# One core, six layers: sums turned by VectorE in two attention layers, projections two batches wide, loads reordered

## Time and profile before

| | |
|---|---|
| median of 3 runs | 1397.02 us (1395.74 to 1397.70) |
| profiled execution, its own time | 1397.33 us |
| its span in the trace | 1395.6 us |
| PE busy | 1329.5 us (95%) |
| DVE busy | 994.2 us (71%) |
| ACT busy | 898.1 us (64%) |
| POOL busy | 603.0 us (43%) |
| mean granted TensorE clock | 0.995 of full speed |

### The profile page before, as it was taken

One profiled execution on the slowest core, in us unless ns is written; L12 is line 12 of the kernel. 1 busy time (PEld: TensorE's weight loads), 2 busy tenths in 40 slices (PEclk: granted clock), 3 DMA queues, 4 the chain that ended last, 5 costly groups with the idle time before them and its releaser, 6 DMA issues.

```text
span 1395.6 us, 46148 instructions
## 1 busy us (share of the span) xinstructions
PE 1329.5 (95%) x20076; PEld 1138.8 (82%) x20076; DVE 994.2 (71%) x1842; ACT 898.1 (64%) x1519; POOL 603.0 (43%) x767
## 2 busy tenths in 40 slices
PE   5999999999999999999999999999999999899997
PEld 4777888777887878888788878888999999778885
DVE  4778777888788777767776788886664446767774
ACT  4777777777777756666566776776434435667764
POOL 4944544576644643443334342222686665111100
PEclk9999999999999999999999999999999999999999
DMA  7211100010100000000000110000000000001000
GB/s 283 76 31 35 31 13 10 24 31 25 38 9 9 10 25 3 3 2 2 3 2 25 33 31 16 9 9 24 9 9 1 2 1 15 10 32 39 17 25 32
DMA packets 16609, 35.11 MB, mean 25 GB/s; under 512 B 2071, under 2 KB 7447, under 8 KB 15895
## 3 DMA queue, kind: packets, MB, share of 16 engines
q1 hardware_dynamic: 16407, 32.16, 7.1%
HBM read 27.96 MB, written 4.19 MB: 23 GB/s over the span
## 4 chain that ended last, share of the span: by engine, by line
PE 67%; DVE 14%; ACT 8%; POOL 5%; issue 3%; DMA 2%; SPq 0%; DVEq 0%; POOLq 0%; ACTq 0%
DVE s_nm L1101 9%; PE ps L717 8%; PE ps L782 8%; PE ps L744 6%; PE ps L796 6%; PE ps L810 6%; PE ps L606 5%; PE ps L659 5%; PE ps L761 5%; PE ps L631 4%; ACT s_PU L952 4%; PE ps L618 4%; PE ps L595 2%; PE ps L722 2%; DVE s_KH L1058 2%
## 5 line engine op out<-in xcount | busy, mean ns | idle before, releaser
L1101 DVE TENSOR_REDUCE s_nm<-ps 128x8 fp32r<-128x960 f32 (+1 forms) x352 | 395.8, 1168 | 88.4 <-PE ps L659 51.0
L952 ACT ACTIVATE s_PU<-ps 120x1024 f32<-120x1024 f32 (+1 forms) x288 | 280.6, 1024 | 105.5 <-PE ps L722 105.3
L717 PE MATMUL ps<-s_Qs,s_KH 32*120 32x256 f32 (+2 forms) x4608 | 184.8, 288 | 6.4 <-ACT s_PU L952 2.6
L1225 POOL TENSOR_TENSOR s_xs<-s_xs,s_rowv 128x512 f32<-128x512 f32 x96 | 123.9, 1291 | 151.8 <-ACT s_nt L857 133.6
L717 PEld LDWEIGHTS ps<-s_Qs,s_KH 32*120 32x120 f32 (+1 forms) x4608 | 151.5, 181 | 28.4 <-issue 5.1
L1254 POOL TENSOR_SCALAR s_rs<-s_mv 128x2 f32<-128x2 f32 x96 | 23.2, 242 | 325.4 <-DVE s_mv L1138 319.8
L961 ACT ACTIVATE s_Os<-ps 128x512 f32<-128x512 f32 x160 | 95.0, 598 | 102.8 <-PE ps L744 64.2
L782 PE MATMUL ps<-s_W,s_oT 128*128 128x256 f32 x960 | 135.3, 291 | 5.2 <-DVE s_oT L1030 3.5
L606 PE MATMUL ps<-s_xT,s_W 128*128 128x256 f32 x960 | 135.9, 292 | 3.1 <-POOL s_xT L1231 2.8
L744 PE MATMUL ps<-s_PU,s_Vp 120*32 120x256 f32 x2048 | 129.5, 384 | 9.2 <-ACT s_PU L952 7.2
L782 PEld LDWEIGHTS ps<-s_W,s_oT 128*128 128x128 f32 x960 | 120.0, 190 | 16.8 <-DVE s_oT L1030 7.0
(11 more groups left out here) (96 smaller groups left out, 2554.4 us busy)
## 6 DMA issues: line engine op xcount, KB each, us to landing
s_cf<-ctx_t SPq DMA_DIRECT2D x32, 240.0 KB, 2.6
s_ws<-weights SPq DMA_DIRECT2D x28, 256.0 KB, 2.7
s_nt<-x_t SPq DMA_DIRECT2D x16, 256.0 KB, 2.6
s_xs<-x_nat SPq DMA_DIRECT2D x4, 1024.0 KB, 11.3
out<-s_xs SPq DMA_DIRECT2D x16, 256.0 KB, 2.0
s_rowv<-rows SPq DMA_DIRECT2D x6, 512.0 KB, 3.9
s_mi<-mask SPq DMA_DIRECT2D x8, 120.0 KB, 3.4
s_who<-who SPq DMA_DIRECT2D x1, 128.0 KB, 3.2
```

What stands on the lines that cost most here:

```text
L717: e.matmul(banks[j][0:n, wide * x:wide * x + wide], kz[row[j], lk, g, c, k0:k0 + n], q[row[j], lq, g, qs_], start=(x == 0 and y_ == 0), st ...
L952: t = e.activation(P_of(i, k)[0:n, :, :], pair("B", i, k)[0:n, :, :], ACT.Exp, scale=0.25)
L1101: e.tensor_reduce(o, v, AX.X, ALU.max, negate=True).then_inc(sem["max"])
L1225: e.tensor_tensor(xs[:, b, :, :], xs[:, b, :, :], row2(layer, 0), ALU.add).then_inc(sem["pool"])
```

## The change

In CROSS and L3 the sums no longer go through PE to be turned. DVE reads each half of PV out of PSUM and turns it in blocks of 32 x 32 (X), which puts 32 rows of each head on partitions; it takes the reciprocals of both halves at once (rec); POOL multiplies all 16 heads (nmul, one 128 x 512 operation); DVE turns back by 32 x 32 blocks out of SBUF (turn, two operations of 128 x 256); then OTh, OTl, O as before, but OTh and OTl read `s_On` in SBUF instead of PSUM. The rows of the two output matrices are permuted on the host (`mixed`). PVe, ON, ONe and OT are gone from these layers.

From CROSS on, T, Q and F1 work for two batches at once: Q is 12 matmuls of 512 columns for a pair, F1 four stages of 12 such matmuls, F2 four stages of 24 matmuls of 256 columns. `s_xT` and `s_Qs` are laid out for pairs.

The weights' low and high parts lie in ten places of one matrix each (three of four matrices before), and a matrix may be prepared when the one that had its place has been read. The high-part buffers change: K0 has 1 instead of 2, `s_oT` 1 instead of 2, `s_Os` 2 whole ones instead of 3 halves, Q 4 instead of 3. The planner waits with the four loads of `x` and with L1's weights; `WANT` has other numbers throughout and `STAY` is 1.453 instead of 0.236, so the order of all layers differs.

```diff
...
+TWOS = ("CROSS", "FFN", "L3")
+TURNED = ("CROSS", "L3")
...
-WSLOT = {n: k % 3 for k, n in enumerate(SETS)}
+
+MATRICES = [(n, m) for n in SETS for m in range(4)]
+PLACE = {x: k % 10 for k, x in enumerate(MATRICES)}
...
-            ON=(3.22, 2.87, 3, 2.88, 0, -1.81), ONe=(1.73, 1.71, -1.22, -2.11, 0, 0.18), OT=(4.46, -4.46, 2.98, 2.5, 0, 3.93),
...
+            exp=(0.82, 14.91, -1.61, 4.93, 0, -24.67), cap=-14.72, PV=(2.7, -1.45, 1.33, 5.16, 0, 6.91), X=(0, 0, 0, -15.84, 0, 2.3),
...
-STAY = 0.236
+STAY = 1.453
...
-        self.ring = {"Q": Slots(3), "KH": Slots(2), "K0": Slots(2), "PU": Slots(7), "Vp": Slots(2), "cT": Slots(2),
-                     "xT": Slots(2), "nt": Slots(2), "ws": Slots(2), "cf": Slots(1), "Os": Slots(3), "On": Slots(1), "oT": Slots(2), "nm": Slots(2), "mT": Slots(2),
+        self.ring = {"Q": Slots(4), "KH": Slots(2), "K0": Slots(1), "PU": Slots(7), "Vp": Slots(2), "cT": Slots(2),
+                     "xT": Slots(2), "nt": Slots(2), "ws": Slots(2), "cf": Slots(1), "Os": Slots(2), "Rc": Slots(2), "On": Slots(1), "oT": Slots(1), "nm": Slots(2), "mT": Slots(2),
...
         if layer == "FFN":
-            for u in range(2):
-                add("PE", "F1", u, after=[x_t] + [("Wl", "F1", m) for m in range(4)],
...
+            for u in range(4 if i == pair else 0):
+                add("PE", "F1", u, after=[x_t, ("Wl", "F1", u)],
+                    rings=[("S", ("F1", i, u), [("Fv", i, 2 * u + 1)]), ("PU", ("F", i, u), [("Hl", i, u)]),
                            ("KH", ("H", i, u), [("F2", i, u)])])
...
+            turned = layer in TURNED
             for hf in range(2):
...
+                    + ([("PV", i, 0)] if hf else []), long=1.36 if self_ else None,
+                    rings=[("MI", ("PV", i, hf), [("X" if turned else "PVe", i, hf)])]
+                    + ([] if hf else [("Os", i, [("turn", i, 0)] if turned else [("ON", i, 0), ("ON", i, 1)])]))
+                if turned:
+                    add("DVE", "X", hf, after=[("PV", i, hf)])
+                else:
+                    add("ACT", "PVe", hf, after=[("PV", i, hf)])
+                    add("PE", "ON", hf, after=[("PVe", i, hf)] + ([("ON", i, 0)] if hf else []),
+                        rings=[("MI", ("ON", i, hf), [("ONe", i, hf)])] + ([] if hf else [("On", i, [("OT", i, 0)])]))
...
+            if turned:
+                add("DVE", "rec", after=[("X", i, 0), ("X", i, 1)], rings=[("Rc", i, [("nmul", i, 0)])])
+                add("POOL", "nmul", after=[("rec", i, 0)])
+                add("DVE", "turn", after=[("nmul", i, 0)], rings=[("On", i, [("OTl", i, 0)]), ("oT", i, [("O", i, 0)])])
+            else:
...
             add("DVE", "OTl", after=[("OTh", i, 0)])
...
-        p.add("SP", "x", k, want=-1 + 1.2 * k)
+        p.add("SP", "x", k, want=-1 + 1.2 * k, after=[("A", 4 * k - 4, 0)] if k else [("K", 0, 0)])
...
-            p.add("SP", "ws", layer, m, want=at, rings=[("ws", (layer, m), [(rest_of(layer), layer, m)])])
+            p.add("SP", "ws", layer, m, want=at, after=[("A", 4 + m, 0)] if layer == "L1" else [], rings=[("ws", (layer, m), [(rest_of(layer), layer, m)])])
...
             def Q(i):
-                m, layer = bankM("Q", i), layer_of(i)
...
                 w.wait_ge(*w_ready(layer, 0))
                 for g in range(2):
                     for c, (cw, cx) in enumerate(PARTS):
                         for k in range(2):
-                            t = e.matmul(m[:, g * 256:g * 256 + 256], wv(layer, cw, 0)[:, k, 128 * g:128 * g + 128], xT_of(i)[:, cx, k, :],
+                            t = e.matmul(v[:, g, :], wv(layer, cw, 0)[:, k, 128 * g:128 * g + 128], xT_of(i)[:, cx, k, :],
                                          start=(c == 0 and k == 0), stop=(c == 2 and k == 1))
...
             def F1(i, u):
-                v, x = pair("F1", i, u), xT_of(i)
...
-                    o = v[:, mt % 4 // 2, 256 * (mt % 2):256 * (mt % 2) + 256]
+                w.wait_ge(*w_ready("F1", u))
+                for h in range(2):
                     for c, (cw, cx) in enumerate(PARTS):
                         for k in range(2):
-                            t = e.matmul(o, wv("F1", cw, mt // 2)[:, k, 128 * (mt % 2):128 * (mt % 2) + 128], x[:, cx, k, :],
+                            t = e.matmul(v[:, h, :], wv("F1", cw, u)[:, k, 128 * h:128 * h + 128], xT_of(i)[:, cx, k, :],
                                          start=(c == 0 and k == 0), stop=(c == 2 and k == 1))
                 t.then_inc(sem["F1"])
...
+                if layer_of(i) in TURNED:
+                    w.wait_ge(sem["turn"], nth("turn", i))
+                    src = On[slot("On", i)][:, :, :].rearrange("p a n -> p (a n)")
...
             def OTlo(i):
...
-                e.tensor_tensor(o[:, 1, :, :].rearrange("p a n -> p (a n)"), bankM("OT", i),
-                                o[:, 0, :, :].bitcast(f32).rearrange("p a n -> p (a n)"), ALU.subtract).then_inc(sem["OTl"])
+                src = On[slot("On", i)][:, :, :].rearrange("p a n -> p (a n)") if layer_of(i) in TURNED else bankM("OT", i)
+                e.tensor_tensor(o[:, 1, :, :].rearrange("p a n -> p (a n)"), src, o[:, 0, :, :].bitcast(f32).rearrange("p a n -> p (a n)"),
+                                ALU.subtract).then_inc(sem["OTl"])
...
+            def X(i, hf):
+
+
+                for x in sums_free(i):
+                    w.wait_ge(*x)
+                w.wait_ge(sem["PV"], nth("PV", i, hf))
+                e.transpose(Os_of(i, hf).rearrange("p g n -> p (g n)"), bankM("PV", i, hf)).then_inc(sem["X"])
+
+            def rec(i):
...
+                e.reciprocal(Rc[slot("Rc", i)][:, :].rearrange("p (h o) -> p h o", o=1), o[:, :, 16:17]).then_inc(sem["rec"])
...
+            def turn(i):
+
+                for x in On_free(i):
+                    w.wait_ge(*x)
+                w.wait_ge(sem["pool"], pool_ops["nmul", i, 0])
+                o = Os[slot("Os", i)]
+                for hf in range(2):
+                    t = e.transpose(On[slot("On", i)][:, hf, :], o[:, 2 * hf:2 * hf + 2, :, 0:16].rearrange("p g m c -> p m g c"))
+                t.then_inc(sem["turn"])
...
+            def nmul(i):
+
+                o = Os[slot("Os", i)][:, :, :, :].rearrange("p g m c -> p (g m) c")
+                w.wait_ge(sem["rec"], nth("rec", i))
...
+                rc = Rc[slot("Rc", i)][:, :].rearrange("p (h o) -> p h o", o=1)
+                e.tensor_tensor(o[:, :, 0:16], o[:, :, 0:16], rc.to_broadcast([128, 32, 16]), ALU.mult).then_inc(sem["pool"])
+
...
+    def mixed(w):
+
+        return w.reshape(2, 2, 4, 16, D).transpose(0, 2, 1, 3, 4).reshape(D, D)
...
```

More of the change, by code:

```diff
@@ L37 @@
+LONG = dict(mci=.5, xT=.6, cT=.6, mi=.6, ws=.6, row=.6, x=.6, out=.6, bo=1.3, N=.72, T=.88, Th=.95, Tl=1.13, Xl=2.6, Q=2.62, Qh=.98, Ql=1.24, K=1.35, K0=.87,
             Kh=1.17, Kl=1.25, V=1.43, Ve=.67, Ch=.5, Cl=1.25, mf=.3, A=.69, max=1.07, M=.22, mTe=.28, B=.95, exp=.91, cap=.67, PV=.87,
-            PVe=.48, ON=.44, ONe=.64, OT=.44, OTh=.48, OTl=.62, O=1.43, y=.6, st=1.05, rs=1.6, ln=.72, lng=2.6, F1=2.86, Fa=.72, Fv=.79,
+            X=.62, rec=.36, nmul=1.3, turn=.68, PVe=.48, ON=.44, ONe=.64, OT=.44, OTh=.48, OTl=.62, O=1.43, y=.6, st=1.05, rs=1.6, ln=.72, lng=2.6, F1=2.62, Fa=.49, Fv=.62,
@@ L276, in make_plan @@
-            last = ("F2", i, 1)
-        else:
-            add("PE", "Q", after=[x_t, (rest_of(layer), layer, 0)],
-                rings=[("MI", ("Q", i, 0), [("Ql", i, 0)]), ("Q", i, [("B", i, u) for u in range(units(i))])])
-            add("ACT", "Qh", after=[("Q", i, 0)] + ([("wa", layer, 0)] if FOLDED[layer] else []))
-            add("DVE", "Ql", after=[("Qh", i, 0)])
+                add("PE", "F2", u, after=[("Hl", i, u), ("Wl", "F2", u)] + ([("F2", i, u - 1)] if u else []),
+                    rings=[] if u else [("MI", ("F2", x, 0), [("y", x, 0)]) for x in two])
@@ new lines, in make_plan @@
+            last = ("F2", pair, 3)
+        else:
+            if i == pair:
+                add("PE", "Q", long=2.62 if len(two) == 2 else 1.43, after=[x_t, (rest_of(layer), layer, 0)],
+                    rings=[(bank, ("Q", i, 0), [("Ql", i, 0)])] + [("Q", x, [("B", x, u) for u in range(units(x))]) for x in two])
+                add("ACT", "Qh", long=LONG["Qh"] if len(two) == 2 else .74, after=[("Q", i, 0)] + ([("wa", layer, 0)] if FOLDED[layer] else []))
+                add("DVE", "Ql", long=LONG["Ql"] if len(two) == 2 else .8, after=[("Qh", i, 0)])
@@ L306, in make_plan @@
                     add("DVE", "max", 2 * u + q, after=[("A", i, u)])
+            for u in range(1, units(i)):
+                p.stages["A", i, u].after.append(("A", i, 0))
             add("PE", "M", after=[("max", i, k) for k in range(2 * units(i))],
@@ L322, in make_plan @@
[L322 to L327 removed]
+                add("PE", "PV", hf, after=[("cap" if self_ else "exp", i, k) for k in half_pairs(i, hf)] + [("Ve", first, 0)]
+                    + ([("PV", i, 0)] if hf else []), long=1.36 if self_ else None,
```

(14 more changed lines are left out.)

338 lines of the change are left out of this document (194 added, 144 removed).

## The result

The changed kernel takes 1372.97 us (median of 4 runs, 1371.68 to 1375.82) against 1397.36 of the kernel before in the same session: ratio 0.983, interval 0.9813 to 0.9848. That is 24.4 us less; 40 were forecast. The profiled execution took 1375.82, the slowest of the four; its span is 1374.1, 21.5 shorter than before.

The account below looks back on a forecast made before the run. PE, busy 95%, was taken to set the pace. CROSS −16.0, L3 −17.2, F1 −8.6, tiling +4.8 and start −3.0 sum to −40.0: 1397.3 becomes 1357 us, range 1335 to 1386.

Parts of the forecast that it names:

- Rival A: In CROSS, DVE operations within SBUF wait for POOL at a shared port: 14.6 us, 1372, or 1386 at twice; chance .2.
- rival D: Width gains nothing and the loads of `x` hid nothing: 3.2, 8.6 and 3.0 us back, at most 1372; chance .1.
- L0 to SELF: First three layers: more changes of tiling on PE cost 4.5 us; moving by more than 10 us would contradict the prediction.
- What leaves PE: In CROSS and L3, 64 ON and 32 OT leave PE: 40.0 us, or 10.0 in eight batches.
- Width: On PE, 512-column matmuls cost .222 each, less than two of 256: Q −3.2 us, F1 −8.6 us.
- DVE becomes the bound: In CROSS, DVE needs 95.1 us per eight batches against PE's 91.0; CROSS gains 8.0 per eight, 16.0 in all.
- Stalls of turn and OTl: On DVE, OTl waits for OTh and turn for nmul; 1.1 us show per two batches, 4.4 in eight.
- L3: Eight batches of L3 take 95.0 us, PE ahead of DVE; gain 8.6 per eight, 17.2 in all.
- The start: Later loads of `x` no longer compete with weights and inputs, halving four waits of PE: −3 us, ends 0 and −5.3.
- rival B: In L0 to SELF the new order fills a third of PE's gaps: −9.5 us, 1347, or 1335 with width; chance .1.
- Costed at nothing: ACT's loss of PVe, POOL's added 1.29 us a batch, single K0 and `s_oT`, and L3's V and O preparation cost nothing.
- Rival C: In CROSS and L3, DVE block transposes cost two passes, X 1.38 and turn .85: 13 us slower, 1411; chance .1.

Follow-up runs that it names:

- narrow: The changed kernel with Q and F1 of the pairs as two matmuls of 256 columns instead of one of 512: 1372.48 us.
- both moved ones: The changed kernel, at five places in CROSS: X ahead of turn and max ahead of OTl, 1388.21 us; the same with O later on PE, 1397.53 us.
- X twice: The changed kernel with every X run twice on DVE, the second behind the first: 1411.46 us.
- X half: The changed kernel with X turning only the first half of its columns from the fifth X on: 1371.03 us.
- refilled: The changed kernel with 12 transposes of a constant on PE ahead of every O of CROSS and L3, 384 in all: 1405.98 us.
- run 208: Not a label of a run: the text says that PE had run 208 matmuls by 34.5 us, against 172 before.
- run 18: Not a label of a run: the text says that over the whole run 18 of 64 turns began while POOL worked.

## Why the prediction was right, and where it was wrong

The time lies in the range and the sign is right; the size is 24 for 40. The time alone would fit rivals A and D as well, at 1372 each; only the rows tell them apart. And one of the prediction's own signs of being wrong was met: L0 to SELF moved by more than 10 us, by 14.8 in the profile and by 11.4 to 15.8 in the traces of all seven kernels here that share its order up to CROSS (the changed one, narrow, both moved ones, X twice, X half, refilled). By its steps:

1. **What leaves PE** (−40.0): right. Put back at the same order, these 40 us cost 33.
2. **Width** (Q −3.2, F1 −8.6): wrong. I took .222 a matmul between .16 and .244; it is .233, and the narrow form in the same order takes the same time. The step that failed is the reasoning from the slow start, "the price scales with PE's own pace": that row shows that PE was slow there, and says nothing of a gain from width. F1 came down by 2.93 − 2.80, 4.2 us in all, most of it without width. For Q I had taken K's 1.43, at 240 columns. In the kernel before, Q at 256 takes 1.61 from start to start ahead of a row-tiled stage (1.51 otherwise):

```profile
831.05 1.68 PE L606 MATMUL ps<-s_xT,s_W 128*128 128x256 f32 x12
832.66 0.97 PE L717 MATMUL ps<-s_Qs,s_KH 32*120 32x256 f32 x24
```

   and a pair takes 2.99 in the changed one, 3.04 in the narrow form:

```profile
860.33 3.05 PE L707 MATMUL ps<-s_xT,s_W 128*128 128x512 f32 x12
863.32 0.97 PE L818 MATMUL ps<-s_Qs,s_KH 32*120 32x256 f32 x24
```

   So Q did save about .2 a pair, some 3 us in all, but hardly by width: that its term comes out is luck. About 4 of the 16 us that are missing are here, in F1, and this half of rival D happened in the main.
3. **CROSS: "DVE becomes the bound"**: wrong in kind, near in size (97.0 for 95.1). The chain runs mostly on PE and passes through ACT and DVE once in two batches. PE's 91.0 was too low by 3.8. Turning and Q left as forecast (10.7 and .9, counted by stage from each start to the next); but A is up by 2.4, PV by 1.4 and M by 1.0. Changes of tiling are 55 in the eight batches before and 64 now, since the work between them was cut finer; the prediction left those of CROSS to idle time. PV's two halves now stand apart, and its group in eight batches of the kernel before:

```profile
L744 PE MATMUL ps<-s_PU,s_Vp 120*32 120x256 f32 x256 | 15.5, 382 | 0.0
```

   and of the changed one, from 827.67 to 924.70:

```profile
L845 PE MATMUL ps<-s_PU,s_Vp 120*32 120x256 f32 x256 | 17.1, 385 | 0.0
```

   is 1.6 us longer. On DVE I had 3.2 too much work and 5.2 too little waiting. With X at half the stretch keeps its length, so DVE alone was not it; X twice and PE refilled show that neither engine has room to spare.
4. **Stalls of turn and OTl**: found where they were put (1.22 and .35 in two batches, 1.6 where 1.1 was forecast). That they could be filled was not claimed, and two runs show that they can't be by these moves.
5. **L3** (−17.2): −18.8. The steady part gave less than forecast, 7.2 in eight batches for 8.6, so that the whole agrees this well is in part luck at its ends.
6. **The start** (−3): PE's idle time in the first 40 us fell from 16.1 to 13.4, about as forecast, but this is no gain in work: by 34.5 us PE had run 208 matmuls against 172 before, by 40 us 270 against 274, with the clock at half from 34. The old places of the loads cost nothing in the time that can be told.
7. **L0 to SELF** (+4.5 of tiling, the start aside): the largest miss, +14.8 for +1.5. PE's idle time is the same (44.6 for 44.5), so rival B, gaps filled by the new order, did not happen; its busy time is up by 754.6 − 739.8 = 14.8. By the windows of 2 us, 8.5 against 1.7 are lost to the clock there: 6.8. The changes of tiling were put at 4.5, which leaves 3.5. By stage, PV is up by 4.7, its halves standing apart as in CROSS (96 groups for 61), and 16 more matmuls that prepare weights of later layers run there, 2.8. Only the clock's part was tried, and with it gone 10.5 of the 14.8 stay. The forecast had no term for the new order but the tiling; what the order itself costs there stays open.
8. **Costed at nothing**: ACT's K0 waited for PE alone and never for Kl, so the single buffer cost nothing where I looked; nmul is cheaper than bo's 1.29.

**Rival A** did not happen in its size, but its mechanism did in part. In eight batches of CROSS turn and OTl, with all operands in SBUF, take 423 and 671 ns beside a POOL that is busy 37.4 of 97 us. Over the whole run 18 of 64 turns began while POOL worked, and they took 400 to 445 ns, as the others (396 to 447): a block transpose did not wait. OTl, which reads two operands from SBUF, did: the four of 32 that began inside one of POOL's products over 128 x 512 took 908 to 1409 and each ended .55 after it, as here:

```profile
953.22 1.29 POOL L1424 TENSOR_TENSOR s_PU<-s_PU 128x512 f32<-128x512 f32 x1 [0.46 <-DVE s_PU L1310]
953.65 1.41 DVE L1134 TENSOR_TENSOR s_oT<-s_On,s_oT 128x512 fp32r<-128x512 f32 x1
```

That is some 2 us in all. In steady CROSS the order lets no OTl begin inside such a product; the rival had taken four exposed operations a batch and chance meetings.

**Rival C**'s premise failed with X at .71. The run with two passes took 1411.46 for the rival's 1411, but that is luck: it doubles X alone, and the rival's sum started from the forecast of 1357. The Trainium skill's 311 ns for a 128x128 block transpose ("VectorE: DVE Perf Modes", section "The three transpose paths", bf16) would make X 1.24 in an estimate of four such; the trace does not agree: .71 for 128x512 in float32, and the measurement decides.
